# Attention on one Trainium2 core: the null value rows, written by GpSimd's copy instead of a TensorE product in each turn

## What is computed

```python
q = (xn @ w_q)...; k, v = jnp.split(xn @ w_kv, 2, axis=-1)
nkv = null_kv.reshape(HEADS, NUM_NULL_KV, 2, DIM_HEAD)
k = jnp.concatenate([nk, k], axis=2)      # 2 null keys ahead of the 1024
v = jnp.concatenate([nv, v], axis=2)      # 2 null values ahead of the 1024
q = _l2norm(q) * q_scale
k = _l2norm(k) * k_scale
sim = q k^T * 8 + alibi, causal mask
out = (softmax(sim) @ v) @ w_out
```

## Time and profile before

| | |
|---|---|
| median of 3 runs | 1947.53 us (1941.84 to 1954.14) |
| the profiled execution, its own time | 1947.45 us |
| its span, first to last instruction | 1945.7 us |
| mean granted TensorE clock | 0.899 |
| first and last null product (L435) | 40.9 and 1148.0 us |
| PE busy | 1656.2 us, 85% of the span |
| POOL busy | 574.1 us, 30% of the span |

### The profile page before, as it was taken

The page is one execution under the profiler, slowest core; times in us unless marked ns, Lnnn a source line. Parts: engine busy times, 40 slices in busy tenths (PEclk is TensorE's granted clock), DMA queues, the critical chain, the costliest instruction groups (busy, mean ns, idle before and its releaser), DMA issues. The chain is left out here.

```text
span 1945.7 us, 28499 instructions
## 1 busy us (share of the span) xinstructions
PE 1656.2 (85%) x8973; PEld 777.5 (40%) x8974; DVE 1088.6 (56%) x2591; ACT 757.8 (39%) x1250; POOL 574.1 (30%) x557
## 2 busy tenths in 40 slices
PE   5899999999999999999999999647964677776777
PEld 2344444444444444443444444345642233232332
DVE  4454665565565555656556547562225766666674
ACT  2445445445444545445444453203422222232231
POOL 4244253253353353353452441160021001110000
PEclk8799999999999999999999999758976777887788
DMA  3602022022022022022021000131110000000000
GB/s 95 184 1 63 1 63 74 1 63 63 2 63 74 1 63 63 1 63 63 1 63 48 17 4 1 48 122 46 47 40 6 6 6 11 11 11 6 0 6 11
DMA packets 106705, 73.63 MB, mean 38 GB/s; under 512 B 5249, under 2 KB 100761, under 8 KB 106318
## 3 DMA queue, kind: packets, MB, share of 16 engines
q1 hardware_dynamic: 104526, 67.76, 11.4%
q0 software_dynamic: 2048, 4.20, 0.7%
HBM read 24.23 MB, written 47.71 MB: 37 GB/s over the span
## 5 line engine op out<-in xcount | busy, mean ns | idle before, releaser
L718 ACT ACTIVATE P<-S,keyb 128x386 f32<-128x386 f32 (+7 forms) x512 | 296.7, 630 | 387.9 <-PE S L514 387.8
L510 PE MATMUL S<-QT,KT 64*128 64x512 f32 (+5 forms) x1792 | 391.0, 492 | 9.5 <-DVE KT L856 7.3
L1036 POOL TENSOR_TENSOR rn<-nm,half 128x12 f32<-128x12 f32 x128 | 295.6, 2314 | 109.0 <-DVE nm L793 109.0
L1052 POOL TENSOR_SCALAR_AFFINE_SELECT P<-P 128x256 f32<-128x256 f32 (+1 forms) x256 | 156.5, 612 | 533.5 <-ACT P L718 533.4
L891 DVE TENSOR_TENSOR Psum<-Psum,P 128x1796 f32<-128x1796 f32 (+7 forms) x256 | 279.2, 1091 | 38.0 <-PE O L534 17.2
L534 PE MATMUL O<-P,V 128*64 128x512 f32 (+5 forms) x1536 | 255.5, 436 | 3.4 <-POOL P L1052 3.4
L510 PEld LDWEIGHTS S<-QT,KT 64*128 64x128 f32 (+1 forms) x1792 | 162.4, 183 | 202.2 <-issue 193.4
L167 POOL TENSOR_TENSOR norm_rstd<-norm_vareps,half 128x4 f32<-128x4 f32 x32 | 32.7, 1023 | 463.8 <-DVE norm_vareps L152 463.7
L405 PE MATMUL W<-xT,wts 128*128 128x512 f32 x256 | 147.1, 672 | 9.4 <-DVE QT L852 6.9
L514 PE MATMUL S<-GQ,GK 64*128 64x512 bf16 (+5 forms) x896 | 153.8, 310 | 0.0
L913 DVE TENSOR_TENSOR part<-W,rden 128x512 f32<-128x512 f32 x128 | 82.5, 686 | 92.6 <-PE W L582 92.6
(11 more groups left out here) (219 smaller groups left out, 2235.9 us busy)
## 6 DMA issues: line engine op xcount, KB each, us to landing
xg<-zero SPq DMA_DIRECT2D x16, 1216.0 KB, 6.9
yg<-zero SPq DMA_DIRECT2D x16, 1216.0 KB, 10.6
wts<-in_w_qkv SPq DMA_DIRECT2D x16, 384.0 KB, 3.8
gu<-in_gu SPq DMA_DIRECT2D x1, 2816.0 KB, 9.5
xb<-xg SPq DMA_DIRECT2D x40, 64.0 KB, 1.8
yg<-yb SPq DMA_DIRECT2D x40, 64.0 KB, 1.6
X<-in_x SPq DMA_DIRECT2D x4, 512.0 KB, 4.4
wo<-in_w_out SPq DMA_DIRECT2D x16, 128.0 KB, 2.3
```

Of the source, the lines that this page charges most:

```text
L510: nc.tensor.matmul(S[hh][0:m, at + c:at + c + w], KT[d, r, p, jt * P:jt * P + m], QT[d, r, p, Q0[jt] + c:Q0[jt] + c + w], start=True, stop ...
L718: nc.scalar.activation(probs(p, jt)[0:m, hh, 0:n], S[hh][0:m, at:at + n], ACT.Exp, bias=keyb[0:m, r, (2 * p + hh) * NKT + jt:(2 * p + hh) ...
L1036: nc.gpsimd.tensor_tensor(rn[:, c, u], nm[:, c, u], powers, ALU.pow).then_inc(rn_ok, 1)
L1052: nc.gpsimd.affine_select(own, own, [[0, 2], [1, w]], ALU.is_ge, 0.0, base=NNULL if jt == 0 else 0, channel_multiplier=-1).then_inc(cut, 1)
```

## The change

The null product of PE is dropped, and the product before it closes its accumulation itself. In its place POOL copies `nvt` (2 x 256) over rows 0 and 1 of tile 0 in `V`, in step 11, behind the cut of that step. It waits for DVE's copy of V0 into `V`, and counts a new semaphore `nv_ok` up, for which PE waits ahead of the first values product of the turn.

```diff
-            tab_ok, nk_ok = s1("tab_ok"), s1("nk_ok")
+            tab_ok, nk_ok, nv_ok = s1("tab_ok"), s1("nk_ok"), s1("nv_ok")
@@ vals (PE)
-                        last = nc.tensor.matmul(o, xT[:, n // NG % 2, jt * P:(jt + 1) * P], wt[:, r, 2 * KW:], start=True, stop=jt > 0)
-                        if jt == 0:
-                            nc.tensor.matmul(o, idf[0:NNULL, :], nvt[:, bass.ds(n % NG, 1), :].rearrange("k a n -> k (a n)"),
-                                             start=False, stop=True)
+                        last = nc.tensor.matmul(o, xT[:, n // NG % 2, jt * P:(jt + 1) * P], wt[:, r, 2 * KW:], start=True, stop=True)
@@ values (PE)
                     if s == 0:
                         pe.wait_ge(prep_ev[BANK["R0"]], emptied(t, "R0"))
                         pe.wait_ge(prep_ev[BANK["V2"]], emptied(t, "V2"))
+                        pe.wait_ge(nv_ok, t + 1)
@@ prepare (POOL)
+                    if s == 11:
+                        null_values(n)
+
+                def null_values(n):
+
+                    pool.wait_ge(prep_ev[BANK["V0"]], emptied(n, "V0"))
+                    nc.gpsimd.tensor_copy(V[0:NNULL, n % 2, 0, :], nvt[:, n % NG, :]).then_inc(nv_ok, 1)
```

## The result

The changed kernel takes 1922.23 us (median of 6 runs, 1916.39 to 1924.58), the kernel before 1947.6 us in the same comparison (1938.49 to 1954.14). The ratio is 0.9874, with an interval of 0.9845 to 0.9902: 1.3% faster, 25 us, nearly twice what was forecast, and outside the stated range.

The account below looks back on a forecast made before the run. PE was taken to set a turn's length. Sixteen turns at 0.82 us less, nothing eaten, copy and wait free, gave 1947.45 - 13.1 = 1934.3 us (chance 0.70), range 1926 to 1945 us.

Parts of the forecast that it names:

- What bounds the kernel; the product: PE sets a turn's length; V0's products go from 1.88 to 1.06 us, saving 0.82 us a turn.
- The split of the 1.06 into 0.63 and 0.43: In V1's two products, the first was put at 0.63 us and the follower of its form at 0.43 us.
- rival 1: V0's null product is worth only its own place: 0.63 us a turn, 1937.4 us, or 0.43, 1940.6 us; chance 0.12.
- Turn 0: Preparation running alone ahead of the attention: its chain goes through V0, so 0.82 us are saved there too.
- Eaten at the turn's end: PE's waits behind V0, for DVE and POOL, would eat nothing of the 0.82 us a turn.
- rival 2: DVE, busy at the turn's end, eats the gain: within 1 us of 1947.5 us, or 1946.6 with turn 0's part; chance 0.09.
- The copy and the wait: POOL's added copy, 0.41 us, lies in an idle gap of 2.59 us; PE's added wait was taken as 0.
- The clock: At turn ends, about as many turns with a fall as before, two more or fewer: 3.4 us either way.
- The price of a fall: A fall of PE's granted clock at a turn's end was put at 1.4 to 1.7 us a turn.
- rival 4: No attention turn has a clock fall any more: twelve turns each 1.6 us shorter, 1915 us; chance 0.05.
- Rival 3: At turn ends the clock stays at 0.50 for three stretches instead of one, 3.4 us a turn: 1982 us; chance 0.04.
- 5 us of scatter: Allowance for run scatter in the range's low end, 1934.3 - 3.4 - 5; 6 us a side was stated before.

Follow-up runs that it names:

- e3_fill: Changed kernel with two more 128-row products in V0, repeating the first and overwriting it: 1943.4 us, ratio 0.9984 to the kernel before.
- e4_pad: Kernel before with its null product padded with rows of zeros to 128 rows: 1935.1 us, ratio 0.9951 to the kernel before.
- e11_after_again: Changed kernel measured once more without any edit: 1921.2 us, ratio 0.9872 to the kernel before.
- e1_no_copy: Changed kernel without POOL's copy of the null values and PE's wait for it, null values left out: 1922.5 us, ratio 0.9883 to the kernel before.
- e8_shorter: Changed kernel without R0's product for the last two tokens' values, DVE copying other data instead: 1908.3 us, ratio 0.9825 to the kernel before.
- e2_both: Changed kernel with PE's null product put back, so product, copy and wait all stand: 1947.9 us, ratio 1.0005 to the kernel before.
- e9_longer: Changed kernel with four more 128-row products in V0: 1962.1 us, ratio 1.0116 to the kernel before.
- e12_order3: Changed kernel with DVE's additions of steps 13 to 15 moved back and 13 small E and R instructions moved to step 13: 1934.5 us, ratio 0.9943.
- e5_busy_before: Kernel before with three idle products in PE's wait for RT, each turn but the last: 1937.2 us, ratio 0.9963 to the kernel before.
- e6_busy_after: Changed kernel with three idle products in PE's wait for RT, each turn but the last: 1923.1 us, ratio 0.9878 to the kernel before.

## Why the prediction was wrong

- **What bounds the kernel; the product.** Right to 0.01 us: 1.88 became 1.06 us. The split of the 1.06 into 0.63 and 0.43 was not right: the rows of e3_fill have 0.54 us for the first product of a group, 0.43 for one in the middle and 0.52 for the last. The total, on which the sum rests, is the same. The lower price of rival 1 (0.43) is what the product would have cost at 128 rows (e3_fill, e4_pad), but as it stood it cost 0.82.
- **Turn 0.** Right: V0 and V1 of the preparation alone, from the first product to the norms, took 2.64 us before (40.37 to 43.01) and 1.82 after (39.96 to 41.78), 0.82 less. That the attention began 1.1 us earlier (71.47 against 72.58 us) shows nothing by itself: in e11_after_again the same changed kernel began at 73.43.
- **Eaten at the turn's end (rival 2).** Right that nothing was. A turn at full clock went from 73.1 to 72.27 us.
- **The copy and the wait.** Right: zero (e1_no_copy). The copy took 0.39 us for 0.41.
- **The clock.** This is the step that failed. The prediction said: "I expect about as many such turns as before, two more or fewer: 3.4 us either way." It was six fewer, and with the less that turns 0 and 1 lost it came to 12 us. The price of a fall was about right (1.4 to 1.7 us said, mostly 1.7 measured). The number was carried over from the kernel before, where it hadn't been counted: the rows show three turns, two of them with a fall, and rival 4 takes twelve of fourteen, where it was eleven. And the same paragraph said that shorter turns would shift it. Rival 4, with a chance of 0.05, went the right way, and its sign was there, turns without a stretch at 0.50; it had all falls gone and 1915 us. Rival 3 (three such stretches for one) was wrong for the changed kernel in turns 1 to 14, but the shape exists: a stretch of 10.2 us stands once in the kernel before and in e8_shorter (between turns 0 and 1), twice in e2_both and three times in e9_longer.
- **Why the number wasn't steady.** The runs show that it goes with the turn's length: 71.8 us two falls, 72.0 three, 72.2 and 72.3 four or five, 72.7 nine, 73.1 eleven or twelve. That half of it is shown for changes of the length that PE's products made, by e2_both and e3_fill from one side and e4_pad and e8_shorter from others. In the kernel before, falls start 75.1 us apart, and a turn with a fall lasts nearly that, so that the next turn's end meets the next fall; the shorter turn breaks that row. This is how the rows look, not a mechanism that a run tested. A law that gives the number for any length isn't shown: e9_longer missed, and e12_order3, with 73.0 us, has eight.

The size of the whole was thus 13 us from PE's order and 12 from the clock. The low end of the range, 1926, also took 5 us of scatter where the paragraph before had set 6; with 6 it would have been 1925, still above the 1922.2 measured. By the profile of before alone one could have seen that the second term was open between +5 us (fourteen falls, three more at 1.7) and -20 us (none); the range should have reached down to 1915.

## What to carry to other kernels

In a loop that PE bounds, whose clock falls once in most rounds, a change of 1% in the length of a round can change how often it falls, and the clock's part can be as large as the edit's own. Price such an edit twice, PE's time and the number of rounds with a fall, and give the second term its full spread. A float32 product with few rows between products of full form cost its own place and two changes of form here, 0.43 + 0.39 us: pad it to the form of its neighbours, or give it to an engine that is idle.

## What the runs showed of the hardware

- At the full clock a float32 product of 128x256 behind another of its form adds 0.43 us; with 2 rows in place of 128 between two such it adds 0.82 us (e4_pad against before).
- POOL copies 2 x 256 float32 in 0.386 us, about as long as its copy of 128 x 4 mostly takes (0.407 us).
- PE's granted clock fell to 1.2 GHz for 3.4 us at a time, now and then for 10.2 us, in eleven of fourteen turns of 73.1 us and in five of fourteen turns of 72.3 us. In the kernel before, PE's longest single wait at a turn's end is 0.92 us. Filling that wait with products of 24 rows didn't change the two numbers (e5_busy_before, e6_busy_after).
